# GRU products of a decoder layer: full products, or pairs of 64-row products in both row halves of the array

## The reference

```
attn    = softmax over slots(q @ k.T), then divided by its sum over the context
updates = attn @ v
gx = updates @ wih.T + bih ; gh = slots @ whh.T + bhh        # three gates each
r = sigmoid(xr + hr) ; z = sigmoid(xz + hz) ; n = tanh(xn + r * hn)
slots = (1 - z) * n + z * slots
```

## Time and profile before

| | us |
|---|---|
| median of 3 runs | 558.18 |
| lowest, highest | 557.22, 720.77 |
| span of the profiled execution | 583.7 |

### The profile page before, as it was taken

How to read it: one execution, slowest core, us unless ns; L and a number is a source line. 1 busy time by engine, 2 the same in 40 slices (tenths; PEclk the granted TensorE clock), 3 DMA queues, 4 the chain that set the end, 5 groups by cost and what they waited for, 6 DMA issues and landing times.

```text
span 583.7 us, 7269 instructions
## 1 busy us (share of the span) xinstructions
PE 518.3 (89%) x2174; PEld 371.6 (64%) x2174; DVE 436.7 (75%) x794; ACT 343.6 (59%) x608; POOL 249.9 (43%) x217
## 2 busy tenths in 40 slices
PE   6999896979789988999999999999899978877773
PEld 2465554637566864788588678858677857655652
DVE  3889999987996679599679859957757758454563
ACT  3548459685984845674567567556566635452333
POOL 0141130503133545548446544824442655545455
PEclk9999997999889998999999999999999999797897
DMA  8950202110101040000000000021120822545331
GB/s 286 321 165 1 72 1 85 59 73 1 44 32 70 1 146 0 2 0 2 1 1 0 0 1 2 1 73 36 36 73 1 298 74 93 146 125 157 114 100 50
DMA packets 28101, 39.98 MB, mean 68 GB/s; under 512 B 7421, under 2 KB 19838, under 8 KB 27776
## 3 DMA queue, kind: packets, MB, share of 16 engines
q1 hardware_dynamic: 24656, 31.10, 17.0%
q0 software_dynamic: 3408, 8.43, 4.0%
HBM read 25.70 MB, written 16.83 MB: 73 GB/s over the span
## 4 chain that ended last, share of the span: by engine, by line
PE 45%; DVE 10%; issue 8%; POOL 4%; another core or an unknown queue 3%; ACT 2%; DMA 1%; SPq 0%; POOLq 0%; DVEq 0%; ACTq 0%
PE psum L1445 31%; PE psum L1535 6%; PE psum L1248 3%; PE psum L1506 2%; PE psum L1333 1%; DVE gru L1858 1%; DVE slots_full L1860 1%; PE psum L1387 1%; DVE gru L1831 1%; POOL sorted_rows L1028 1%; POOL gru L998 1%; DVE gru L1838 1%; DVE slots_lo L1681 1%; POOL out L1036 1%
## 5 line engine op out<-in xcount | busy, mean ns | idle before, releaser
L1445 PE MATMUL psum<-slots_hi,w_hh 128*128 128x512 f32 x560 | 182.1, 407 | 6.6 <-DVE gru L1831 6.6
L1445 PEld LDWEIGHTS psum<-slots_hi,w_hh 128*128 128x128 f32 x560 | 104.3, 191 | 34.1 <-DVE gru L1831 8.1
L998 POOL TENSOR_TENSOR gru<-slots_full,gru 128x512 f32<-128x512 f32 x43 | 65.7, 1528 | 116.1 <-ACT gru L751 116.1
L1445 PE MATMUL psum<-slots_lo,w_hh 128*128 128x512 f32 x280 | 112.2, 401 | 0.0
L1445 PE MATMUL psum<-at,v_ih_pair 128*128 128x512 f32 x288 | 91.3, 401 | 3.1 <-DVE at L1737 3.1
L751 ACT ACTIVATE gru<-gru,vec 128x512 f32<-128x512 f32 x48 | 34.6, 722 | 63.9 <-DVE gru L1838 63.5
L1831 DVE SCALAR_TENSOR_TENSOR gru<-psum,vec,gru 128x512 f32<-128x512 f32 x48 | 35.9, 748 | 41.4 <-PE psum L1445 31.7
L1445 PEld LDWEIGHTS psum<-at,v_ih_pair 128*128 128x128 f32 x288 | 53.9, 190 | 19.6 <-DVE at L1737 3.4
L1131 PE MATMUL psum<-early_hi,w_in 128*128 128x512 f32 x128 | 58.1, 613 | 5.2 <-DMA early_hi<-in_xT 5.1
L1445 PEld LDWEIGHTS psum<-slots_lo,w_hh 128*128 128x128 f32 x280 | 53.5, 191 | 12.9
L1535 PE MATMUL psum<-slots_full,w_tile 128*128 x156 | 51.1, 459 | 9.8 <-DVE w_tile L2079 6.5
(11 more groups left out here) (249 smaller groups left out, 882.5 us busy)
## 6 DMA issues: line engine op xcount, KB each, us to landing
gathered<-sorted_rows SPq DMA_DIRECT2D x39, 129.0 KB, 1.5
x_scratch<-slots_full SPq DMA_DIRECT2D x8, 512.0 KB, 3.0
x_block<-x_scratch SPq DMA_DIRECT2D x8, 512.0 KB
early_hi<-in_xT SPq DMA_DIRECT2D x3, 1024.0 KB, 5.5
x_tm<-in_x SPq DMA_DIRECT2D x4, 512.0 KB, 7.5
slots_full<-expert_plus SPq DMA_DIRECT2D x1, 2048.0 KB
sorted_rows<-gru SPq DMA_DIRECT2D x1, 1032.0 KB, 12.2
early_hi<-in_xT SPq DMA_DIRECT2D x2, 512.0 KB, 4.5
```

Of the source, the lines that this page charges most:

```text
L998: pool.tensor_tensor(DF(u), full[:, c, seq(k, h), blk(j)], X(u), ALU.subtract).then_inc(d_pool, 1)
L1445: last = pe.matmul(psum[:, bank, :], w, d, start=start and i == 0, stop=stop and i == len(pairs) - 1, skip_group_check=begun or late)
```

## The change

In steps 1 to 4 all units but the first (k = 1, q = 0) and the last (k = 4, q = 7) are given by `split_unit`: 30 units. Each 128-row product becomes two of 64 rows, one on partitions 0 to 63 ("low") and one on 64 to 127 ("high"), into the same bank at different times. `both` issues low and high products in turn, the low ones of one gate beside the high ones of an earlier gate, in another bank; the high products of XN and z are issued in the next unit. Of the update of a gate the half that holds the low part of `at` takes one product instead of two: low*low is left out. Banks of r and HN rotate over 0, 4 and 1. `mean_squares` stands after the first products of HN, `sums` behind all low products of unit 5. In the last split unit (k = 4, q = 6) XN and z are full products again. In the old `unit`, HN waits for `r_act` instead of `t_dve`, and r for `t_dve` instead of `r_act`.

```diff
-        R_B, Z_B, HN_B, XN_B, S_B = 0, 2, 4, 5, 6
+        Z_B, XN_B, S_B = 2, 5, 6
+        TURNS = (0, 4, 1)
...
+        def r_bank(u):
+            return TURNS[2 * u % 3]
+
+        def hn_bank(u):
+            return TURNS[(2 * u + 1) % 3]
...
-                        pe.wait_ge(r_act, u - 1)
+                        pe.wait_ge(t_dve, u - 1)
...
-                        run(R_B + u % 2, hidden(0), stop=False)
+                        run(r_bank(u), hidden(0), stop=False)
                     if late:
-                        pe.wait_ge(t_dve, u)
-                        run(HN_B, hidden(2)).then_inc(hn_mm, 1)
+                        pe.wait_ge(r_act, u)
+                        run(hn_bank(u), hidden(2)).then_inc(hn_mm, 1)
                         pe.wait_ge(z_act, u - 1)
                         run(Z_B + u % 2, hidden(1), stop=False)
                     if q % U == 0:
                         pe.wait_ge(at_lo, 2 * k + h + 1)
-                    run(R_B + u % 2, update(0), start=False).then_inc(r_mm, 1)
+                    run(r_bank(u), update(0), start=False).then_inc(r_mm, 1)
                     if "R" in between:
                         between["R"]()
                     if not late:
                         if u > 0:
-                            pe.wait_ge(t_dve, u)
+                            pe.wait_ge(r_act, u)
                         else:
                             pe.wait_ge(res_done, H2 * B)
-                        run(HN_B, hidden(2)).then_inc(hn_mm, 1)
+                        run(hn_bank(u), hidden(2)).then_inc(hn_mm, 1)
...
+                def both(lows, highs):
+                    low = high = None
+                    for i in range(max(len(lows), len(highs))):
+                        if i < len(lows):
+                            bank, w, d, start = lows[i]
+                            low = pe.matmul(psum[:, bank, :], w, d, start=start, stop=False, skip_group_check=True)
+                        if i < len(highs):
+                            bank, w, d, start = highs[i]
+                            high = pe.matmul(psum[:, bank, :], w, d, start=start, stop=True, skip_group_check=True)
+                    return low, high
+                def split_unit(k, q, before, between=None, last=False):
+                    h, j, c = place(q)
+                    b, u = seq(k, h), QU * k + q
+                    n_split = u - QU
+                    between = between or {}
+                    r, hn, z, a = r_bank(u), hn_bank(u), Z_B + u % 2, at[(2 * k + h) % 3]
+                    lo, hi = half(0), half(1)
+                    x_before, z_before = before
+                    def cols(gate):
+                        return slice(gate * D + c * P, gate * D + (c + 1) * P)
+                    def hidden(bank, gate, rows):
+                        return [(bank, wh[w][rows, i, cols(gate)], slots[d][rows, i, b, blk(j)],
+                                 rows == lo and (i, w, d) == (0, 0, 0)) for i in range(C) for w, d in PASSES]
+                    def update(bank, gate, rows):
+                        return [(bank, vp(w, b)[rows, cols(gate)], a[rows, blk(j)],
+                                 rows == lo and gate == 2 and w == 0) for w in range(2 if rows == half(h) else 1)]
+                    r_lo, r_new, hn_lo = hidden(r, 0, lo), update(r, 0, lo), hidden(hn, 2, lo)
+                    r_hi, hn_hi = hidden(r, 0, hi) + update(r, 0, hi), hidden(hn, 2, hi)
+                    n = 4 - len(r_new)
+                    pe.wait_ge(t_dve, u - 1)
+                    if u == QU + U:
+                        pe.wait_ge(x1_lo, 2 * H2)
+                    if q == 0:
+                        pe.wait_ge(s_hi, NB * (k - 1))
+                        pe.wait_ge(s_lo, NB * (k - 1))
+                    if x_before:
+                        pe.wait_ge(x_low, n_split - 1)
+                    low, high = both(r_lo[0:2], x_before)
+                    if x_before:
+                        high.then_inc(xn_mm, 1)
+                        pe.wait_ge(z_low, n_split - 1)
+                    both(r_lo[2:], z_before[0:4])
+                    if q % U == 0:
+                        pe.wait_ge(at_lo, 2 * k + h + 1)
+                    low, high = both(r_new, z_before[4:4 + len(r_new)])
+                    low.then_inc(r_low, 1)
+                    pe.wait_ge(r_act, u)
+                    low, high = both(hn_lo[0:n], z_before[4 + len(r_new):])
+                    if z_before:
+                        high.then_inc(z_mm, 1)
+                    if "R" in between:
+                        between["R"]()
+                    pe.wait_ge(r_low, n_split)
+                    pe.wait_ge(z_act, u - 1)
+                    z_lo = [] if last else hidden(z, 1, lo)
+                    lows = hn_lo[n:] + z_lo
+                    low, high = both(lows[0:4], r_hi[0:4])
+                    low.then_inc(hn_low, 1)
+                    n = len(r_hi)
+                    low, high = both(lows[4:n], r_hi[4:])
+                    high.then_inc(r_mm, 1)
+                    pe.wait_ge(hn_low, n_split)
+                    pe.wait_ge(t2_dve, u)
+                    if not last:
+                        lows = lows[n:] + update(XN_B, 2, lo)
+                        low, high = both(lows, hn_hi[0:len(lows)])
+                        low.then_inc(x_low, 1)
+                        low, high = both(update(z, 1, lo), hn_hi[len(lows):])
+                        low.then_inc(z_low, 1)
+                        high.then_inc(hn_mm, 1)
+                        if "XN" in between:
+                            between["XN"]()
+                        return update(XN_B, 2, hi), hidden(z, 1, hi) + update(z, 1, hi)
+                    low, high = both([], hn_hi)
+                    high.then_inc(hn_mm, 1)
+                    for w in range(2):
+                        mm = pe.matmul(psum[:, XN_B, :], vp(w, b)[:, cols(2)], a[:, blk(j)], start=w == 0, stop=w == 1,
+                                       skip_group_check=True)
+                    mm.then_inc(xn_mm, 1)
+                    pairs = [(wh[w][:, i, cols(1)], slots[d][:, i, b, blk(j)]) for i in range(C) for w, d in PASSES]
+                    pairs = pairs + [(vp(w, b)[:, cols(1)], a[:, blk(j)]) for w in range(2)]
+                    for i, (w, d) in enumerate(pairs):
+                        mm = pe.matmul(psum[:, z, :], w, d, start=i == 0, stop=i == len(pairs) - 1,
+                                       skip_group_check=True)
+                    mm.then_inc(z_mm, 1)
+                    return [], []
...
+                rest = [], []
                 for k in range(1, LAST):
-                    unit(k, 0)
-                    unit(k, 1)
-                    unit(k, 2, {"HN": lambda: mean_squares(k + 1)})
+                    if k == 1:
+                        unit(k, 0)
+                    else:
+                        rest = split_unit(k, 0, rest)
+                    rest = split_unit(k, 1, rest)
+                    rest = split_unit(k, 2, rest, {"R": lambda: mean_squares(k + 1)})
                     scores(k + 1)
-                    unit(k, 3)
-                    unit(k, 4)
-                    unit(k, 5, {"XN": lambda: sums(k + 1)})
-                    unit(k, 6)
+                    rest = split_unit(k, 3, rest)
+                    rest = split_unit(k, 4, rest)
+                    rest = split_unit(k, 5, rest, {"XN": lambda: sums(k + 1)})
+                    rest = split_unit(k, 6, rest, last=k + 2 == PAIRS)
                     if k + 2 < PAIRS:
-                        unit(k, 7)
+                        rest = split_unit(k, 7, rest)
...
-                    dve.scalar_tensor_tensor(out=X(u), in0=psum[:, HN_B, :], scalar=col(c, V_BHH + 2), in1=X(u),
+                    dve.scalar_tensor_tensor(out=X(u), in0=psum[:, hn_bank(u), :], scalar=col(c, V_BHH + 2), in1=X(u),
...
```

More of the change, by code:

```diff
@@ L167, in decoder_layer @@
         d_pool, e_dve, s_dve = sem("d_pool"), sem("e_dve"), sem("s_dve")
+        r_low, hn_low, x_low, z_low = sem("r_low"), sem("hn_low"), sem("x_low"), sem("z_low")
         ss_mm, ss_ln, rstd_done = sem("ss_mm"), sem("ss_ln"), sem("rstd_done")
@@ L744, in r_gate @@
                         act.wait_ge(s_dve, u - 2)
-                    act.activation(X(u), psum[:, R_B + u % 2, :], ACT.Sigmoid,
+                    act.activation(X(u), psum[:, r_bank(u), :], ACT.Sigmoid,
                                    bias=brz[:, c, 0:1]).then_inc(r_act, 1)
@@ L1318, in _ @@
                 for q in range(2):
-                    first_hidden(q, 0, R_B + q)
+                    first_hidden(q, 0, r_bank(q))
                 first_hidden(0, 1, Z_B)
@@ L1364, in token_bank @@
                     if n == 30:
-                        pe.wait_ge(t_dve, UL + QU)
+                        pe.wait_ge(r_act, UL + QU)
                     if n == 31:
@@ L1417, in ranks @@
                     if RANK_AFTER[g] is None:
-                        pe.wait_ge(r_act, UL + QU - 1)
```

(3 more changed lines are left out.)

## The result

The changed kernel takes 572.04 us (median of 4 runs, 570.92 to 574.06), the kernel before 557.70 beside it (median of 4, of which one took 720.77): a ratio of 1.0257 [1.0234, 1.0281], slower by 14.3 us. The forecast was 567.5 (549 to 592).

A forecast was written before the change was run, and what follows sets the result against it. PE's chain of products was taken to bound steps 1 to 4, its time counting one for one. The terms 0 + 4.7 - 1.7 + 3.0 + 2.3 + 1.2 = +9.5 on 558.2 gave 567.5 us, range 549 to 592.

The forecast's parts named there:

- the likeliest case (561 to 574): The forecast's own case for the whole kernel: chance 0.42, of which 0.27 up to 569.3 (within 2%) and 0.15 slower.
- Places: Split units on PE: 24 product places before and after, each costing 0.233 us, so 0 us for 720 places.
- the cheap place: Rival for split units: a place costs 0.216 to 0.220 us, -10 to -12 from places, total 556 to 562; chance 0.18.
- the dear one: Rival: two weight loads don't fit a place, which costs 0.245 to 0.28 us; +9 to +34, total 576 to 600; chance 0.13.
- The rival of drift: Rival: each half takes products in its own order, 22.5 places paid at 0.216 us, total 545; chance 0.11.
- The scores: Steps 2, 3 and 4: late r delays Ln, PE stands 1.72 us before the scores; +1.56 each, +4.7.
- The attention for the next step: The r update at the next step's start waits for late attention: +1.0 for each of steps 2, 3 and 4, +3.0.
- `sums`: On PE, now between 64-row products: four times two changes of tile size at 0.10 to 0.19 us, +1.2.
- XN, Z and the rotating banks: Units without a stall: DVE and ACT free these some eight places before they are needed, 0 us.
- Step 1: PE's first stall for L1831 goes, the second is replaced; scores at 229.8 instead of 231.52: -1.7 us.
- The drain: The last split unit takes 34 places on PE: +2.3 us.
- The rival that the clock falls at the new stalls at the scores: Rival: PE's clock falls behind each new stall at the scores, +4.5 us, total 572; chance 0.09.

The follow-up runs named there:

- e6: The kernel before, unchanged, run again for a second profile: 559.10 us, ratio 1.0020.
- e3: The changed kernel with ACT's table load, Ln, Exp and next load put ahead of the sigmoid of r in unit 2: 564.64 us, ratio 1.0146.
- e10: e3 with the low*high half products of the split units' updates left out as well as low*low: 565.22 us, ratio 1.0102.
- e4: e3 with the next step's normaliser ahead of unit 6's sigmoid of r, and attention and its spreading ahead of unit 6's candidate: 570.36 us, ratio 1.0236.
- e7: The changed kernel, unaltered, run again for a second profile: 571.97 us, ratio 1.0247.
- e2: The changed kernel with the low*low half products put back: 575.74 us, ratio 1.0335.
- e5: The changed kernel with the low*high half products of the split units' updates left out as well as low*low: 575.38 us, ratio 1.0333.
- e8: The changed kernel with the low*low half products put back, a second run, beside e7: 574.39 us, ratio 1.0309.

## Why the prediction came out as it did

The side, the mechanism and the likeliest case (561 to 574) were right. The time lies in the upper part of that case, which had the smaller chance (0.15 against 0.27), as the size was +9.5 where +14.3 was measured. The stretch from the scores of step 0 to the gate mean accounts for the most of it. Starts on PE:

| | scores, step 0 | scores, step 1 | scores, step 4 | gate mean | whole |
|---|---|---|---|---|---|
| before, first profile (clock fell in step 1) | 184.87 | 231.52 | 386.33 | 413.29 | 228.42 |
| before, e6 | 188.02 | 233.13 | 387.95 | 414.92 | 226.90 |
| changed kernel | 189.09 | 233.82 | 398.76 | 428.31 | 239.22 |
| e3 | 187.31 | 230.75 | 390.41 | 420.02 | 232.71 |

Against e6, which like the changed kernel had no fall of the clock there, it is +12.3. Point by point:

- **Places: 0 predicted, and 0 came.** The distance is 0.233 and two loads fit: the cheap place, the dear one and missing overlap are out. The rule behind my count, the sum of the longer lists, is not right, as e10 shows: 21.7 were paid where that rule gives 23 and the longer half of the unit 21. Here both give 24. The rival of drift is half true: the halves shift by one product, but the longer one has 24 in every unit, and they don't even out over several units as that rival needed. The rule of the Trainium skill that a load overlaps a product only in another row group (TensorE: Matmul & The Clock Gate, Packing small matmuls), by which by my estimate some 77 us would have gone, is not borne out: full products of one row group cost 0.233, and pairs no less.
- **The scores: +1.56 a step predicted.** The idle is 1.68 where PE lost 0.16 before, so 1.52. e3 confirms the cause.
- **The attention for the next step: +1.0 predicted.** 324.38 - 323.11 - 0.233 = 1.04, and 0.10 in the first product behind it: 1.14. This is read from the rows; no run takes this wait away alone.
- **`sums`: 0.3 each predicted, 0.38 measured.** 0.08 before it (309.33 - 309.02 - 0.233), 0.20 in it (310.46 - 309.33, less 4 * 0.233) and 0.10 behind.
- **"XN, Z and the rotating banks ...: 0" failed.** The low products of HN of a unit overwrite the bank that the sigmoid of r of the unit before has to read. PE in unit 5 of step 2, and ACT there:

```profile
299.51 0.39 PE L1505 MATMUL psum<-at,v_ih_pair 64*128 64x512 f32 x1
299.83 0.49 PE L1505 MATMUL psum<-slots_hi,w_hh 64*128 64x512 f32 x1
...
300.17 0.39 PE L1505 MATMUL psum<-slots_hi,w_hh 64*128 64x512 f32 x1
```

```profile
298.15 1.06 ACT L774 ACTIVATE sq_block<-slots_full 128x1024 f32<-128x1024 f32 x1 [2.65 <-DVE slots_full L1969]
299.12 0.67 ACT L753 ACTIVATE gru<-psum,brz 128x512 f32<-128x512 f32 x1
```

  The squares wait 2.65 us for DVE with the sigmoid behind them; it ends at 299.79 and PE goes on 0.04 later. 300.17 - 299.51 is 0.66 for two places, 0.2 too many, and the same comes at 311.97: 0.4 a step. I counted places from the bank's release and not what stands ahead of that release on ACT. e4 shows how much more this wait can cost.
- **Together**, a step takes 54.98 - 51.61 = 3.37 more (predicted 2.86; the four terms sum to 3.44), three times 10.1 instead of 8.6.
- **Step 1: -1.7 predicted, and this is the largest miss.** What I worked out for the changed kernel came true: means 37.8 us after the scores of step 0 (measured 37.67), scores 7.1 behind them (7.06). But I set it against a profile of before in which the clock had fallen. Against e6 it is 44.73 - 45.11 = -0.4. With the fall in both (the first profile, 46.65, and e7, 234.50 - 188.16 = 46.34) it is -0.3. The fall is no part of the change, and I booked its absence as a gain. The forecast also says that PE waits once in the four steps; the profile has two waits, 4.0 us together, both in step 1, and this term counts both.
- **The drain: 2.3 + 0.3 for the last `sums` predicted.** Scores of step 4 to the gate mean: 29.55 - 26.97 = 2.6.
- **About 2 us stay open**: 14.3 less 12.3. The profiled executions themselves, 572.78 and e6's 559.64, lie only 13.1 apart: 12.3 in this stretch, 1.1 ahead of it and -0.3 behind. The other 1.2 is how these two differ from the medians. The start of the stretch moves from 184.9 to 189.1 over all the kernels, the unchanged one too, and no pair of profiles pins a difference of 2 us there.

The rival that the clock falls at the new stalls at the scores did not happen in the changed kernel: in both its profiles the bursts behind the 1.7 us stalls take 3.65. It did in e2, e5 and e8, at 5.35 - 3.65 = 1.7 us each where 1.5 was predicted.

## What to carry to other kernels

Count the longer half of a packed flow, unit by unit: products taken out of the shorter one bring nothing, unless someone waits for their result, and those taken out of the longer one bring time only as far as the other engines and the clock follow (e10: 1.5 us in one step, nothing in the next). When products are interleaved, a result gets ready as late as its last piece; follow each such signal through the queue of the engine that it releases, where a table load or a transcendental may stand behind it, and move those ahead first. Before a term is read from a profile, look whether that stretch had an event of its own, such as a fall of the clock, and take a second profile of the unchanged kernel if it did.

## What was not expected of the hardware

Packed halves keep their own pace (e10, above): the low half's product 0.07 behind a lone high one, and a high product started 0.23 ahead of a low one that stands before it in the program.

The clock reacts to stalls near 1.7 to 1.9 us, but not to each. The eight bursts of scores in the two profiles of the changed kernel, behind idles of 1.7, took 3.65 us at a granted clock of 1.00. Of the twelve of e2, e5 and e8, behind 1.9, six took 5.35 us (one, three and two), the first of e5 at a mean of 0.68, so largely at the lower of the two levels, 1.2 GHz. Behind waits of 1.7 to 1.8 for the attention it fell two times out of three in e10 (269 and 375 us) and in e5. But behind e4's three waits of 2.5 us it stayed at 1.00, and in step 1 of e7 it was 0.50 from 227 to 230, behind waits of 1.0 and 1.1 that the first profile of the same kernel passed at 1.00. So the length of the idle alone doesn't decide it, and what does stays open.
